# The first head's row of negated maxima made in two halves, and the order of the first attention unit written out as one list

## The reference

```
q, k, v = h1 @ wq, h1 @ wk, h1 @ wv                # h1: the normalized, modulated x
scores  = einsum("bhqd,bhkd->bhqk", q, k) / 8
attn    = softmax(scores, axis=-1)
out     = einsum("bhqk,bhkd->bhqd", attn, v)
```

## Time and profile before

| | us |
|---|---|
| median of 3 runs | 1208.64 (1204.94 to 1209.55) |
| the profiled execution | 1206.21 |
| its span | 1204.4 |
| PE busy | 1116.7 |
| DVE busy | 859.7 |
| POOL busy | 695.7 |
| ACT busy | 591.8 |

### The profile page before, as it was taken

The page is one execution under the profiler, slowest core; times in us unless marked ns, Lnnn a source line. Parts: engine busy times, 40 slices in busy tenths (PEclk is TensorE's granted clock), DMA queues, the critical chain, the costliest instruction groups (busy, mean ns, idle before and its releaser), DMA issues.

```text
span 1204.4 us, 30646 instructions
## 1 busy us (share of the span) xinstructions
PE 1116.7 (93%) x12739; PEld 730.9 (61%) x12739; DVE 859.7 (71%) x1685; ACT 591.8 (49%) x855; POOL 695.7 (58%) x641
## 2 busy tenths in 40 slices
PE   4789999999999999999999999899899979999996
PEld 1255656656656657656666566567667756656664
DVE  5667767667667567677686676848868966786876
ACT  3345545544453444444444445544444544257677
POOL 6657866755655667677676556436535633433433
PEclk7799999999999999999999999999999989999999
DMA  8240220220210202202202203122533343000001
GB/s 285 53 123 2 54 54 3 54 53 3 54 35 21 55 2 54 54 2 54 54 2 54 54 2 89 36 59 58 137 77 80 65 127 123 1 1 9 15 14 36
DMA packets 41854, 63.52 MB, mean 53 GB/s; under 512 B 11459, under 2 KB 22383, under 8 KB 41461
## 3 DMA queue, kind: packets, MB, share of 16 engines
q1 hardware_dynamic: 40413, 60.91, 20.2%
q10 hardware_dynamic: 1304, 0.66, 0.2%
HBM read 20.63 MB, written 2.10 MB: 19 GB/s over the span
## 4 chain that ended last, share of the span: by engine, by line
PE 69%; DVE 16%; ACT 5%; DMA 4%; issue 4%; POOL 1%; SPq 1%; DVEq 0%; ACTq 0%
PE outs L810 9%; PE scores L869 8%; PE scores L870 7%; PE mixed L831 7%; PE outs L787 5%; PE scores L931 5%; DVE maxes L1801 4%; PE outs L894 4%; PE outs L892 4%; PE outs L893 4%; PE outs L945 4%; PE outs L820 3%; DVE exps_rest L1824 3%; DMA head_operands<-neg_max_rows 2%; PE outs L844 2%
## 5 line engine op out<-in xcount | busy, mean ns | idle before, releaser
L1533 POOL TENSOR_TENSOR exps_rest<-exps 128x1024 f16<-128x1024 f32 (+1 forms) x297 | 510.3, 1723 | 310.3 <-ACT exps L1207 309.3
L1207 ACT ACTIVATE exps<-scores 128x1024 f32<-128x1024 f32 (+1 forms) x320 | 297.0, 937 | 258.6 <-PE scores L870 239.7
L1801 DVE TENSOR_REDUCE maxes<-mixed 128x1 f32<-128x512 f32 x512 | 334.6, 684 | 91.9 <-PE mixed L831 87.8
L892 PE MATMUL outs<-values,exps 128*128 128x65 f16 (+1 forms) x2176 | 227.1, 193 | 1.6 <-POOL exps_rest L1533 1.6
L893 PE MATMUL outs<-values,exps 128*128 128x64 f16 (+1 forms) x2176 | 227.2, 192 | 0.0
L894 PE MATMUL outs<-values,exps_rest 128*128 128x65 f16 (+1 forms) x2176 | 227.0, 194 | 0.0
L869 PE MATMUL scores<-head_operands 128*128 128x512 f16 (+1 forms) x576 | 219.4, 381 | 7.1 <-DMA head_operands<-neg_max_rows 6.4
L870 PE MATMUL scores<-head_operands 128*128 128x512 f16 (+1 forms) x576 | 219.1, 380 | 0.0
L892 PEld LDWEIGHTS outs<-values,exps 128*128 128x128 bf16 (+1 forms) x2176 | 201.8, 98 | 22.2 <-POOL exps_rest L1533 2.7
L893 PEld LDWEIGHTS outs<-values,exps 128*128 128x128 bf16 (+1 forms) x2176 | 200.7, 98 | 23.9
L894 PEld LDWEIGHTS outs<-values,exps_rest 128*128 128x128 f16 (+1 forms) x2176 | 200.6, 97 | 0.0
(11 more groups left out here) (200 smaller groups left out, 1597.3 us busy)
## 6 DMA issues: line engine op xcount, KB each, us to landing
head_operands<-qk_pairs SPq DMA_DIRECT2D x128, 256.0 KB, 4.5
head_operands<-qk_pairs SPq DMA_DIRECT2D x32, 128.0 KB, 2.5
stage<-in_L_xcond_ff_w_dram SPq DMA_DIRECT2D x3, 1024.0 KB, 5.3
residual<-in_x_dram SPq DMA_DIRECT2D x4, 512.0 KB, 9.8
stage<-in_L_ffn_w_dram SPq DMA_DIRECT2D x2, 1024.0 KB, 5.0
head_operands<-in_x_dram SPq DMA_DIRECT2D x1, 2048.0 KB, 9.4
out_dram<-out_tile SPq DMA_DIRECT2D x16, 128.0 KB, 1.7
attn_outT<-in_L_xcond_attn_wq_dram SPq DMA_DIRECT2D x1, 1024.0 KB, 8.2
```

Of the source, the lines that this page charges most:

```text
L892: mm(o, eb[:, sl], vb[:, DH:VW], start=(kt == 0 and q == 0), stop=False, skip_group_check=True)
L1207: A(E[0:a.ks, c % RING, 0:n], SP_[c % 2][0:a.ks, 0:n], ACT.Exp, scale=SCALE).then_inc(s.exps, 1)
L1533: G.tensor_tensor(R[0:a.ks, c % RING, 0:n], e, e.bitcast(BF16).rearrange("p (n two) -> p n two", two=2)[:, :, 1], ALU.subtract).then_inc(s ...
L1801: V.tensor_reduce(mx[:, h, t, kh:kh + 1], m[:, :], AX_X, ALU.max).then_inc(s.maxed, 1)
```

## The change

The first row is made in two halves. When the first 8 `max` of head 0 (query tiles 0 to 3) are reduced, DVE negates the maximum of those four tiles, and a new item `first` transposes them, copies them and sends them (1 KB) with semaphores of its own. The `row` of head 0 does the same later for tiles 4 to 7. The first chunk of scores waits for `first` alone, chunk 4 (the second half of the queries) for the other half. All other rows are as before.

The order from the first `max` to the end of unit 0 is now a written-out list, `FIRST_UNIT`, taken by `self_unit()`. In it 9 `max` stand before the first `v`, one between the two `v`, two before the first `scores`, and the last four among the first chunks of scores; the `max` of head 1, the projections of unit 1 and the rest are spread singly as in `SELF_UNIT`. Between row 1 and chunk 8 stand now three `values`, four `max` and the transposes of one `normT`, where there were one `values`, two `max` and one `normT`.

```diff
--- before.py
+++ after.py
@@ -55,6 +55,28 @@
 Q_HI, Q_LO, K_HI, K_LO = range(4)
 
 
+FIRST_UNIT = (
+    ("max", 0, 0, 0), ("max", 0, 0, 1), ("max", 0, 0, 2), ("max", 0, 0, 3), ("max", 0, 0, 4), ("max", 0, 0, 5),
+    ("max", 0, 0, 6), ("max", 0, 0, 7), ("max", 0, 0, 8), ("setup", "rows"), ("v", 0, 0), ("first", 0, 0),
+    ("max", 0, 0, 9), ("v", 0, 1), ("setup", "columns"), ("max", 0, 0, 10), ("max", 0, 0, 11), ("scores", 0),
+    ("rest", 0), ("max", 0, 0, 12), ("scores", 1), ("max", 0, 0, 13), ("max", 0, 0, 14), ("q", 1, 0),
+    ("scores", 2), ("max", 0, 0, 15), ("max", 0, 1, 0), ("rest", 1), ("values", 0), ("q", 1, 1), ("rest", 2),
+    ("row", 0, 0), ("max", 0, 1, 1), ("scores", 3), ("max", 0, 1, 2), ("values", 1), ("max", 0, 1, 3),
+    ("k", 1, 0), ("setup", "tokens8"), ("scores", 4), ("max", 0, 1, 4), ("max", 0, 1, 5), ("rest", 3),
...
+    ("max", 1, 0, 12), ("values", 10), ("max", 1, 0, 13), ("max", 1, 0, 14), ("values", 11), ("max", 1, 0, 15),
+    ("scores", 13), ("scores", 14), ("max", 1, 1, 0), ("rest", 12), ("row", 1, 0), ("values", 12),
+    ("max", 1, 1, 1), ("scores", 15), ("rest", 13), ("rest", 14), ("max", 1, 1, 2), ("max", 1, 1, 3),
+    ("values", 13), ("out", 0, 0), ("max", 1, 1, 4), ("scores", 16), ("rest", 15), ("max", 1, 1, 5),
+    ("values", 14), ("values", 15), ("max", 1, 1, 6), ("max", 1, 1, 7), ("out", 0, 1))
...
-    def self_unit(self, a, g):
+    def self_unit(self, a, g, order):
 
         stage = g // 4
         pieces = {0: ("norm1", "normT1", "hi1", "lo1"), 2: ("projB", "norm", "normT", "hi", "lo")}.get(stage, ("projA",))
-        for kind, *at in SELF_UNIT:
-            if kind in ("scores", "rest", "values"):
+        for kind, *at in order:
+            if (g, kind, at) == (0, "scores", [0]):
+                self.self_at = len(self.steps) + 1
+            if kind == "setup":
+                self.add("setup", what=at[0])
+            elif (g, kind, at[0]) == (0, "v", 0):
+                self.add("item", 0, 0, (kind, at[1]), bank=(2, 4)[at[1]])
+            elif kind in ("scores", "rest", "values"):
                 self.add(kind, 0, g + at[0] // a.chunks, c=at[0] % a.chunks)
             elif kind == "slot":
                 self.notes(g, at[0])
-            elif kind in ("q", "k", "v", "row", "out", "max"):
+            elif kind in ("q", "k", "v", "row", "out", "max", "first"):
                 what = (kind, at[1]) if kind != "max" else ("max", at[1], at[2] // 2, at[2] % 2)
                 self.add("item", 0, g + at[0], what)
             elif kind in pieces:
...
-        for what in m[0]:
-            self.add("item", 0, 0, what)
-        self.add("setup", what="rows")
-        self.add("item", 0, 0, ("row", 0))
-        first_item("v", 0, 2)
-        first_item("v", 1, 4)
-        self.add("setup", what="columns")
-        self.add("scores", 0, 0, c=0)
-        self.self_at = len(self.steps)
 
         n = [[("max", h, t, 0) for t in range(2)] for h in range(2)]
         self.boundary = {2: [(0, ("q", 0))], 3: [(0, ("q", 1))], 4: [(0, ("k", 0))], 6: [(1, ("q", 0))],
                          7: [(1, ("q", 1))], 8: [(1, ("k", 0))], 9: [(0, n[0][0])], 10: [(0, n[0][1]), (0, n[1][0])],
                          11: [(0, ("row", 0)), (0, n[1][1])], 12: [(0, ("row", 1)), (0, ("v", 0))]}
         for g in range(UNITS):
-            if g in (0, UNITS - 1):
-                self.unit(a, g, slots if g else first)
+            if g == UNITS - 1:
+                self.unit(a, g, slots)
             else:
-                self.self_unit(a, g)
+                self.self_unit(a, g, SELF_UNIT if g else FIRST_UNIT)
...
+        def first_tile(ai, g, what):
+
+            return TPH if (ai, g, what) == (0, 0, ("row", 0)) else 0
 
         def queries(a, g, which):
 
@@ -837,7 +860,11 @@
                                       start=True, stop=True)
                 elif kind == "row":
                     pe.wait_ge(s.negmax, CREDIT + 2 * g + what[1] + 1)
-                    last = tr(m[0:TPB, 0:P], nm[:, what[1], :], identf[:, :])
+                    t0 = first_tile(ai, g, what)
+                    last = tr(m[0:TPB - t0, 0:P], nm[:, what[1], t0:TPB], identf[:, :])
+                elif kind == "first":
+                    pe.wait_ge(first_negmax, 1)
+                    last = tr(m[0:TPH, 0:P], nm[:, 0, 0:TPH], identf[:, :])
                 else:
                     pe.wait_ge(s.summed, CREDIT + 4 * g + 3 + what[1])
                     for i in range(TPH):
@@ -859,7 +886,9 @@
                     pe.wait_ge(emb_rows, 4)
                 if ai == 1 and c % 2 == 0:
                     pe.wait_ge(s.summed, CREDIT + 4 * g + c - 2 if g or c else CREDIT)
-                if c % (2 * a.groups) == 0:
+                if (ai, g, c) == (0, 0, 0):
+                    pe.wait_ge(first_loaded, 16)
+                elif c % (2 * a.groups) == 0 or (ai, g, c) == (0, 0, a.groups):
                     pe.wait_ge(s.rows[h], 16 * (g + 1) + CREDIT)
...
@@ -1186,10 +1215,16 @@
                     if ai == 1 and g == 0:
                         act.wait_ge(AT[0].sem.rows[what[1]], 16 * UNITS + CREDIT)
                     act.wait_ge(s.rows[what[1]], 16 * g + CREDIT)
-                    A(nmT[:, what[1], :], m[0:TPB, 0:P], ACT.Copy).then_inc(s.row, 1)
+                    t0 = first_tile(ai, g, what)
+                    A(nmT[0:TPB - t0, what[1], :], m[0:TPB - t0, 0:P], ACT.Copy).then_inc(s.row, 1)
                     act.wait_ge(s.row, CREDIT + 2 * g + what[1] + 1)
-                    act.dma_start(HB[DH:DH + 1, par, what[1], QM, :].rearrange("a (t q) -> a t q", t=TPB),
-                                  nmT[:, what[1], :]).then_inc(s.rows[what[1]], 16)
+                    act.dma_start(HB[DH:DH + 1, par, what[1], QM, t0 * P:S].rearrange("a (t q) -> a t q", t=TPB - t0),
+                                  nmT[0:TPB - t0, what[1], :]).then_inc(s.rows[what[1]], 16)
+                elif kind == "first":
+                    A(nmT[0:TPH, 2, :], m[0:TPH, 0:P], ACT.Copy).then_inc(first_row, 1)
+                    act.wait_ge(first_row, 1)
+                    act.dma_start(HB[DH:DH + 1, 0, 0, QM, 0:HALF].rearrange("a (t q) -> a t q", t=TPH),
+                                  nmT[0:TPH, 2, :]).then_inc(first_loaded, 16)
...
@@ -1809,8 +1844,12 @@
                             dve.wait_ge(AT[0].sem.row, CREDIT + 2 * UNITS)
                         dve.wait_ge(s.row, CREDIT + 2 * g + h - 1)
                         dve.wait_ge(s.maxed, 2 * a.max_items * g + a.max_no(what) + 1)
-                        V.tensor_reduce(nm[:, h, :], mx[:, h, :, 0:a.max_parts], AX_X, ALU.max,
+                        t0 = first_tile(ai, g, ("row", h))
+                        V.tensor_reduce(nm[:, h, t0:TPB], mx[:, h, t0:TPB, 0:a.max_parts], AX_X, ALU.max,
                                         negate=True).then_inc(s.negmax, 1)
+                    if (ai, g, what) == (0, 0, ("max", 0, TPH - 1, 1)):
+                        dve.wait_ge(s.maxed, 2 * TPH)
+                        V.tensor_reduce(nm[:, 0, 0:TPH], mx[:, 0, 0:TPH, :], AX_X, ALU.max, negate=True).then_inc(first_negmax, 1)
```

More of the change, by code:

```diff
@@ L160, in add @@
             self.items[ai] += 1
-            bank = bank or self.bank(what[0] in ("max", "row"))
+            bank = bank or self.bank(what[0] in ("max", "row", "first"))
         elif kind in ("proj", "normT") and bank is None:
@@ L286, in attention @@
             k += n
-        first = [[(0, i) for i in m[1][3 * c:3 * c + 3]] for c in range(5)] + [[(0, m[1][15])], [(0, ("row", 1))]]
-        first += [[] for _ in range(a.chunks - 6)]
         put(slots, 5, 0, ("row", 1))
-        own = [len(s) for s in slots]
         for i, what in enumerate([("q", 0), ("q", 1), ("k", 0), ("k", 1)]):
```

15 lines of the change are left out of this document (13 added, 2 removed).

## The result

| | before | with the change |
|---|---|---|
| median of 20 runs, us | 1208.55 (1203.63 to 1211.87) | 1199.97 (1195.15 to 1205.68) |
| ratio, 95% interval | | 0.9938 (0.9924 to 0.9951) |
| span of the profiled execution, us | 1204.4 | 1200.9 |

The change makes the kernel faster by 0.62%, 7.5 us with 5.9 to 9.2 by the interval (the two medians as they stand are 8.6 apart). The forecast was 5 us less, 1203.6 us. The measured median, 1199.97, lies inside the range of 1198.8 to 1208.2 and the direction is right; that the change would stay within 0.5% was given the larger chance, 0.59, and did not come.

The account below looks back on a forecast made before the run. Before the first scores, DVE was taken to bound the `max` stretch and PE, half of it at 1.2 GHz, the products of v after it. Terms -5.3 + 1.0 - 0.6 = -4.9, so -5 us: 1203.6 us, range 1198.8 to 1208.2.

Parts of the forecast that it names:

- The stretch of `max`: Head 0's 16 `max` before the first scores: DVE was said to bound them, busy throughout at 0.69 us each.
- POOL costs nothing: POOL's part of the chunks is 32.7 of unit 0's 52.4 us and starts earlier with the scores: no cost.
- Term 1: First `max` to first scores: scores start at 54.5 instead of 59.85, -5.3 us.
- Term 2: Four `max` and one transpose moved behind the first scores: +1.0 us on PE.
- Term 3: Waits and seams from first scores to unit 1's second chunk: 7.2 us instead of 7.8, -0.6 us.
- The remaining 5.5: Unit 0's waits from DVE and seams, apart from transfers: 5.0 us before, taken as 5.5 with the change.
- A: Unit 0's waits fall to those of unit 1, 4.2 us instead of 7.2: -8, 1200.6 us; chance 0.25.
- B: Before the first scores the clock rises late, at 57.8 as before: -2.3, 1206.3 us; chance 0.2.
- D: Slower: single `max` and waits keep the clock at 1.2 GHz beyond 57.8; 1215 us; chance 0.05.
- C: DVE takes PE's place in unit 0, each `max` waiting 0.1 us: about -1, 1207.6 us; chance 0.08.

Follow-up runs that it names:

- warm_after: The changed kernel with 18 idle products on PE just before the first `max`, their result thrown away; ratio 0.9976 to the kernel before.
- half_alone: The kernel before with the first row in halves and the new order up to the first scores, unit 0 then by the old loop; ratio 0.9962.
- columns_late: The changed kernel with v's weights made earlier, v before the first `max`, and the setup columns behind the first scores; ratio 0.9971 to the kernel before.
- order_alone: The changed kernel's written-out list with the first row whole again behind all 16 `max`; ratio 0.9963 to the kernel before.
- tokens_spread: The changed kernel with the four DVE operations of the setup `tokens8` placed singly among the steps of unit 0; ratio 0.9933 to the kernel before.

## Why the prediction was right, and where it fell short

**The mechanism** was right in its main steps. The first scores now wait for eight reductions instead of sixteen, and after them PE was the bound; the clock rose early, with v; unit 1 kept its length; the parts stand alone and add. The size was short by 2.5 us, a third of the whole, in terms 1 and 3. Two readings were incomplete without harm. The stretch of `max` is not DVE's alone: at full clock the same reductions follow at 0.60 us instead of 0.69 (warm_after), so PE's half clock has a share in it. And "POOL costs nothing" looked at the chunks only; GpSimd ended the weights of v 0.14 us before v began, which was luck, and where it was not so, in half_alone, v waited 0.44 us for them, though the first scores still came after 11.73.

**Term 1, to the first scores**: -5.3 forecast, -6.0 measured. Two sizes were off. The landing of the half row was put at 2.7 us after the issue, between 1.5 and 3.09; it is 1.71 and was no bound. I leaned to the row that had company, head 1's. The Trainium skill's fixed cost of about 2.0 us (DMA: Bandwidth & Descriptors, on the anatomy of one DMA) was nearer. That section gives it for transfers that GpSimd issues, and the rows are issued by ScalarE. Without other transfers under way it was 1.71 for 1 KB (columns_late), near their end 1.68 for 2 KB (half_alone), and beside them 3.1, so page and trace come near each other for the quiet case only. And v, `first` and `max` took 50.68 to 53.37, 2.7 us, where I had 3.3: the clock rose 2.2 us after v began, before the first v had ended, where I had taken the 3.3 us of the kernel before.

**Term 2, the moved `max`**: +1.0 forecast. order_alone and the change differ by 50.85 - 49.49 = 1.4 in unit 0, so 1.0 is about right, with some 0.4 more in DVE's waits.

**Term 3, the waits**: -0.6 forecast. Now 50.85 - 45.6 = 5.2 us are waits and seams, where I had 7.2; against the 7.8 of before that is -2.6. This is the step that failed in size. Of the 7.2 I had put 1.7 on transfers: 0.6 for head 1's row, 0.9 for unit 1's operands, 0.2 for the second half row. None of the three appears. I had counted only PE's steps as their cover and added DVE's waits beside them; but a wait for a maximum that lies between issue and use is cover too. The k of unit 1 ended at 72.36; after it PE waited 0.57 for a maximum, and the first `max` of unit 1 at 80.09 has no wait for the transfers left. For head 1's row the cover was 3.9 us, from 80.51 to 84.43, where I had 3.3 and a need of 3.8. That this cover, and not some faster transfer, took the waits away is read from the trace; order_alone shows that the order does it. The remaining 5.5 were 5.2, though DVE's load rose as forecast (41.66 us busy; 41.4 forecast).

**The rivals.** A (waits as in unit 1, -8) was nearest in size, yet its reason holds in part: seams and DVE's waits stayed at 5.2 against 4.2. B and D did not occur in the change; D did in columns_late. C, DVE takes PE's place, is refuted for the change: 2.5 us of waits for maxima in unit 0 are more than the 1.8 of before by 0.7 only, and tokens_spread, which eased DVE, won 0.4 in unit 0.

**The chances.** A quarter of the forecast and A went past 0.5%, 0.36 in all. With the three transfer waits counted as covered the sum would have been -6.6 and that side the likelier.

## What to carry to other kernels

Where a row of numbers for all queries gates the first product, cut it at the size that the first consumer needs: the second half then hides under work that PE had to do anyway, and the extra transfer cost nothing here, with 2.2 us between issue and use where 1.84 were needed. Count more where other transfers are under way: head 1's row took 3.09 us among them and 1.68 at their end. In a sum of waits, don't add the waits of one chain to those of another that runs beside it: what PE loses to DVE between a transfer's issue and its use is that transfer's cover. And a head start bought by taking dense work out of a stretch can be paid back in TensorE's clock, so read the granted clock of the stretch behind it.
